# A normalization's root of variance worked out from the one before it, and its scaling given to ACT

## Chip, cores, metric

The kernel runs on one core of one Trainium2 chip. The metric is the device time of one execution in microseconds (us); a version's time is the median of its runs. Engines are named as the profile does: PE (TensorE), DVE (VectorE), ACT (ScalarE), POOL (GpSimd) and SP (SyncE, which here only issues transfers).

## What is computed

The input is 8 batches of 512 tokens with 128 features, float32. Four blocks follow each other: two attentions and two feed-forward parts, each added to its input and then normalized per token. The change touches the first attention alone:

```python
def _layernorm(x, axis=-1, eps=1e-05):
    m = jnp.mean(x, axis=axis, keepdims=True)
    v = jnp.var(x, axis=axis, keepdims=True)
    return (x - m) / jnp.sqrt(v + eps)

# first attention, per batch
q, k, v = jnp.split(jnp.einsum('bsd,ed->bse', x, w_qkv), 3, axis=-1)
att = jax.nn.softmax(jnp.einsum('bqd,bkd->bqk', q, k) * DIM ** -0.5, axis=-1)
y = jnp.einsum('bqk,bvd->bqd', att, v)          # sum over k and, apart from it, over v
h = x + jnp.einsum('bqd,ed->bqe', y, w_fc) + b_fc
a = (h - mean(h)) * rsqrt(var(h) + 1e-5) * gamma + beta   # first normalization
x = _layernorm(x + a)                                      # second
# the next block begins with
h = ln1_scale * (x - mean(x)) / sqrt(var(x) + EPS) + ln1_shift   # third, its scale applied in the next phase
```

The einsum that multiplies att by v sums over k in att and over v in v separately, so y is the row's sum of att times one vector.

## The kernel before

The program is a row of phases, each ended by a barrier; the first, `phase_attention`, works on one batch of 512 tokens (four row blocks of 128, `NT = 4`) per step, eight steps n = 0 to 7, the last two written out behind a loop of three turns with two steps each. Buffers are double by s, the step's parity. Each engine runs its own sequence in the order written; semaphores tie them together.

- SP, per step: waits for `x_free`, issues the load of x for tile n+2, waits for `x1_ready` and stores x1, waits for `z1_ready` and stores z1. A load stands behind the z1 store of the step before it.
- PE, per step n: four scores (`ps[4+i]`, each freed by the exp of the tile before), then `front(n+1)`: four transposes of x (L278), the projections q (L281) and k (L282), then the sum for v (L297) and the output weight (L299).
- ACT, per step: four exps (L319, each waiting for its negated maximum from DVE), `front(n+1)`: xT (L309), q (L311), k (L313); then vsum (L324), then four att (L329), which give only the row sums `attsum` that DVE needs, after waiting for DVE's `rinv`.
- POOL: `norm.root`, that is eps added to four variances per partition (L116) and a power of -0.5 (L119), three times per step; between them `add_bfc` (xb, L247) and `add_beta` (xbeta, L253) for the next tile.
- DVE, `sequence`: `rinv` (L352); maxima 0 and 1 of tile n+1 (L342, L344); h from PSUM (L361); its bn_stats and bn_aggr (L105, L111); maxima 2 and 3; the first normalization `norm.apply` (L132, four instructions of 128x128, one per row block); times gamma (L372); plus xbeta (L374); moments; x1 by `norm.apply`; moments; z1 by `norm.apply`.

`Norm.moments`, `Norm.root` and `Norm.apply` are shared by the phases, so their lines (L105 to L132) occur with the names of several tiles; `a_` marks this phase, and in the profile a_x stands for x1 and for the loaded x, a_h for h and h2, a_z for z1.

## Time and profile before

| | us |
|---|---|
| three runs | 2220.67, 2200.15, 2215.17 (median 2215.17) |
| the profiled execution | 2213.47 |
| its span, first to last instruction | 2212.0 |
| DVE busy | 1324.4 (60%) |
| PE busy | 1545.4 (70%) |
| ACT busy | 1029.8 (47%) |
| POOL busy | 345.8 (16%) |
| first phase: first instruction of the next phase (SP) | 184.03 |

Times in the rows are in us from the span's start; a row of the timeline has start, duration, engine, line, operation, what it writes and reads, shape and count, and in brackets the engine's idle time before it with what ended it. The granted clock (PEclk) is a share of 2.4 GHz. The shares above are means over all phases and say little of the first; its own are read by step.

### The profile page before, as it was taken

How to read it: one execution, taken by the hardware profiler on the slowest of the kernel's cores; microseconds unless marked ns; L12 is line 12 of the kernel's file. 1: busy time of each engine (PE TensorE's matmuls, PEld its weight loads, DVE VectorE, ACT ScalarE, POOL GpSimd, SP SyncE). 2: the span in 40 equal slices, each digit the busy share in tenths (PEclk: the TensorE clock that was granted, in tenths of full speed). 3: DMA queues.
4: the chain of work that ended last, by engine and by line, in shares of the span. 5: the costliest groups of instructions: out<-in, count | busy, mean ns of one | idle time of the engine just before them, and what ended most of it. 6: DMA issues, size and time to landing. Idle time of an engine off the chain costs nothing. (4 is left out here: it accounts for less than half of the span.)

```text
span 2212.0 us, 53944 instructions
## 1 busy us (share of the span) xinstructions
PE 1545.4 (70%) x18859; PEld 988.0 (45%) x19047; DVE 1324.4 (60%) x3180; ACT 1029.8 (47%) x1964; POOL 345.8 (16%) x633
## 2 busy tenths in 40 slices
PE   5532447777722999997525888887878787888447
PEld 2211224444422666664212655555545555555323
DVE  4774277667445676664421766575756575677546
ACT  4332316666700323321414776575757566676203
POOL 2232325555432000000210000000000000000013
PEclk8766659999955999998865999798989898999759
DMA  1114722222146122121888999999999999999442
GB/s 38 43 39 142 235 56 63 62 54 70 29 127 218 51 77 81 52 105 35 245 217 302 334 363 361 351 344 333 344 341 346 336 343 344 338 341 349 126 134 57
DMA packets 194998, 432.92 MB, mean 196 GB/s; under 512 B 37776, under 2 KB 86576, under 8 KB 185360
## 3 DMA queue, kind: packets, MB, share of 16 engines
q1 hardware_dynamic: 171376, 248.53, 36.9%
q10 hardware_dynamic: 12672, 152.05, 16.5%
q0 software_dynamic: 10720, 29.11, 5.1%
q8 instruction: 164, 2.69, 0.5%
q14 instruction: 66, 0.54, 0.1%
HBM read 225.80 MB, written 203.55 MB: 194 GB/s over the span
## 5 line engine op out<-in xcount | busy, mean ns | idle before, releaser
L2083 DVE CUSTOM_DVE_ANT_0 r_shifted<-r_ps_ac,r_shifted 128x512 f32<-128x512 f32 x512 | 352.1, 688 | 319.9 <-PE r_ps_ac L1960 137.1
L2049 ACT ACTIVATE r_probs<-r_ps_keys 128x512 f32<-128x512 f32 x512 | 309.6, 605 | 265.9 <-PE r_ps_keys L1967 233.6
L1967 PE MATMUL r_ps_keys<-r_ident,r_shifted 128*128 128x128 f32 x2048 | 333.0, 288 | 69.6 <-DMA r_v<-v 36.6
L2028 ACT ACTIVATE r_wide<-r_ps_wide 128x512 f32<-128x512 f32 (+1 forms) x576 | 329.7, 591 | 79.4 <-PE r_ps_wide L1951 78.8
L1967 PEld LDWEIGHTS r_ps_keys<-r_ident,r_shifted 128*128 128x128 f32 x2048 | 273.4, 149 | 50.5 <-issue 9.8
L1951 PE MATMUL r_ps_wide<-r_r,r_qv 48*32 48x64 bf16 (+12 forms) x6144 | 239.0, 256 | 62.3 <-issue 49.4
L2091 DVE TENSOR_SCALAR r_shifted<-r_shifted,r_mx 128x512 f32<-128x512 f32 x512 | 249.2, 487 | 18.3
L860 ACT ACTIVATE c_probs<-c_ps_keys 128x512 f32<-128x512 f32 (+1 forms) x384 | 174.7, 530 | 149.6 <-PE c_ps_keys L786 149.4
L1951 PEld LDWEIGHTS r_ps_wide<-r_r,r_qv 48*32 48x32 bf16 x6144 | 103.7, 95 | 165.1 <-issue 163.8
L1427 ACT ACTIVATE e_silu<-e_ps_a 128x1024 f32<-128x1024 f32 x64 | 65.7, 1027 | 216.1 <-PE e_ps_a L1360 216.1
L923 DVE TENSOR_REDUCE c_mx_off<-c_ps_rows 128x2 f32<-128x768 f32 (+2 forms) x192 | 120.8, 686 | 63.7 <-PE c_ps_rows L757 63.7
L1960 PE MATMUL r_ps_ac<-r_k,r_qu 128*128 128x512 bf16 x325 | 134.2, 413 | 34.5 <-issue 27.7
L1978 PE MATMUL r_ps_out<-r_probs,r_v 128*9 128x128 f32 x4096 | 147.7, 281 | 15.2 <-issue 14.5
L124 POOL MEMSET n_norm_consts<- 128x4 f32 x1 | 0.1, 102 | 942.7 <-POOLq L1791 942.7
L757 PE MATMUL c_ps_rows<-c_qk 48*128 48x128 bf16 (+2 forms) x896 | 76.5, 257 | 88.0 <-DVE c_mx_off L923 41.6
L1500 DVE TENSOR_TENSOR e_gu<-e_silu,e_ps_b 128x1024 f32<-128x1024 f32 x64 | 78.2, 1221 | 94.3 <-PE e_ps_b L1360 94.3
L1360 PE MATMUL e_ps_a<-e_hT_half,e_w_half 128*128 128x512 f32 x384 | 125.7, 462 | 4.3 <-DVE e_w_half L1555 4.3
L1960 PEld LDWEIGHTS r_ps_ac<-r_k,r_qu 128*128 128x128 bf16 x512 | 49.4, 97 | 169.4 <-issue 123.6
L891 POOL TENSOR_SCALAR_AFFINE_SELECT c_probs<-c_probs 128x256 f32<-128x256 f32 x256 | 98.4, 409 | 154.5 <-ACT c_probs L860 154.1
L1978 PEld LDWEIGHTS r_ps_out<-r_probs,r_v 128*9 128x9 f32 x4096 | 102.3, 92 | 42.8 <-issue 30.8
L1375 PE MATMUL e_ps_o<-e_weighed,e_w 128*128 128x512 f32 x256 | 120.5, 594 | 0.0
L786 PE MATMUL c_ps_keys<-c_qk 50*128 50x512 bf16 (+3 forms) x512 | 93.8, 311 | 27.5 <-ACT c_probs L860 20.1
(201 smaller groups left out, 2138.0 us busy)
## 6 DMA issues: line engine op xcount, KB each, us to landing
skew<-r_wide ACTq DMA_DIRECT2D x64, 2224.0 KB, 11.9
r_shifted<-skew SPq DMA_DIRECT2D x64, 2048.0 KB, 17.0
e_weight_all<-weights SPq DMA_DIRECT2D x8, 2048.0 KB, 7.6
c_qk<-qk_stacks POOLq DMA_DIRECT2D x64, 192.0 KB, 3.7
stack<-d_part SPq DMA_DIRECT2D x96, 128.0 KB, 2.7
qk_stacks<-b_part SPq DMA_DIRECT2D x48, 128.0 KB, 3.4
qk_stacks<-b_part POOLq DMA_DIRECT2D x48, 128.0 KB, 3.7
stack<-d_part POOLq DMA_DIRECT2D x48, 128.0 KB, 4.0
```

Of the source, the lines that this page charges most:

```text
L860: act.activation(probs[:, p, e, at:at + width], ps_keys[f % BANKS][:, 0:width], ACT.Exp, scale=SCALE)\
L923: last = dve.tensor_reduce(off[:, :, NT * p + b], ps[:, :, at:at + width], AX_X, ALU.max)
L1360: last = pe.matmul(ps[:, k, :], w[a][:, e, k * P:(k + 1) * P], hT_halves[b][:, s, :], start=(i == 0), stop=(i == 2))
L1375: last = pe.matmul(ps_o[s][:, :], w3[:, e, k * P:(k + 1) * P], weighed[:, e % 4, k, :], start=(e == 0 and k == 0), stop=(e == NE - 1 and k ...
L1951: last = pe.matmul(ps[Q * a:Q * a + Q, frm - lo:to - lo], qv[rows, h, q0 + one:q0 + one + Q], r[rows, g // 2, h, at:at + to - frm], start= ...
L1960: pe.matmul(ps_ac[u % 2][:, :], qu[:, s, h, b * P:(b + 1) * P], k[:, s, h, :], start=True, stop=True)\
L1967: last = pe.transpose(ps_keys[u % 2][:, j * P:(j + 1) * P], shifted[:, s, u, j * P:(j + 1) * P], ident[:, :])
L1978: last = pe.matmul(ps_out[Q * b:Q * b + VW, h * P:(h + 1) * P], v9[:, s, j, h * VW:(h + 1) * VW], probs[:, h % 2, j, b * P:(b + 1) * P], s ...
L2028: act.activation(wide[:, s, c, lo:hi], ps_wide[bk % BANKS][:, 0:hi - lo], ACT.Copy).then_inc(wide_sb, 1)
L2049: act.activation(probs[:, h % 2, :, b * P:(b + 1) * P], ps_keys[u % 2][:, :].rearrange("p (j i) -> p j i", j=NT), ACT.Exp, scale=SCALE).th ...
L2083: dve.tensor_tensor_reduce(out=shifted[:, s, u, :], in0=ps_ac[u % 2][:, :], in1=shifted[:, s, u, :], scale=1.0, scalar=LOWEST, op0=ALU.add ...
L2091: dve.tensor_scalar(shifted[:, s, u, :], shifted[:, s, u, :], mx[:, u:u + 1], None, ALU.subtract).then_inc(s_ready, 1)
```

## The change

Let v be the variance that the second normalization finds. Its output x1 has mean 0 and variance v/(v+eps), so the third one's factor per row is 1/sqrt(v * rstd^2 + eps). The new kernel works this out on POOL (`find_factor`: square of rstd, times v, plus eps, power -0.5) and ACT multiplies x1 by it (`scale_rows`, four ACTIVATE with a scale per row), one step later, between vsum and att. DVE's third moments and third apply are gone. The first normalization is now two groups of scalar_tensor_tensor: (h - mean) * gamma, then * rstd + xbeta, each four instructions of 128x128. The second normalization has its own `Norm` object, `norm2`. The maxima stand differently: three before h and the fourth behind the second moments. The first two steps are written out ahead of the loop, which makes two turns.

On DVE, one step from h to its second apply; the names are tiles, a_ps the score banks in PSUM. Before:

```order
L361 SCALAR_TENSOR_TENSOR a_h<-a_ps,a_attsum,a_xb 128x128 x4
L51 ISA
L105 BN_STATS a_norm_stats<-a_h 128x6 x4
L108 ISA
L111 BN_AGGR a_norm_mv<-a_norm_stats 128x2 x4
L341 REGISTER_ALU
L342 TENSOR_REDUCE a_mx<-a_ps 128x1
L344 TENSOR_SCALAR a_negm<-a_mx 128x1
L341 REGISTER_ALU
L342 TENSOR_REDUCE a_mx<-a_ps 128x1
L344 TENSOR_SCALAR a_negm<-a_mx 128x1
L132 TENSOR_SCALAR a_h<-a_h,a_norm_mv,a_norm_rstd 128x128 x4
```

The same place in the changed kernel (second step, written out):

```order
L389 SCALAR_TENSOR_TENSOR a_h<-a_ps,a_attsum,a_xb 128x128 x4
L105 BN_STATS a_norm_stats<-a_h 128x6 x4
L111 BN_AGGR a_norm_mv<-a_norm_stats 128x2 x4
L398 SCALAR_TENSOR_TENSOR a_h<-a_h,a_norm_mv,a_gam 128x128 x4
L405 SCALAR_TENSOR_TENSOR a_h<-a_h,a_norm_rstd,a_xbeta 128x128 x4
L105 BN_STATS a_norm_stats<-a_h 128x6 x4
L111 BN_AGGR a_norm_mv<-a_norm_stats 128x2 x4
L370 TENSOR_REDUCE a_mx<-a_ps 128x1
L372 TENSOR_SCALAR a_negm<-a_mx 128x1
L132 TENSOR_SCALAR a_x<-a_h,a_norm_mv,a_norm_rstd 128x128 x4
```

No maximum stands between the first moments and the first normalization now; the one left behind h (the fourth) comes after the second bn_aggr, and the third has gone ahead of h.

On ACT, from the last exp of a tile to the att of that tile; a_z is the new group. Before:

```order
L319 ACTIVATE a_probs,a_rowsum<-a_ps,a_negm 128x512
L308 REGISTER_ALU
L309 ACTIVATE a_xT,a_xsum<-a_ps 128x512
L310 ISA
L311 ACTIVATE a_qT<-a_ps 128x512
L312 REGISTER_ALU
L313 ACTIVATE a_kT<-a_ps 128x512
L324 ACTIVATE a_vsum<-a_ps 128x128
L329 ACTIVATE a_att,a_attsum<-a_probs,a_rinv 128x512 x4
```

Now:

```order
L337 ACTIVATE a_probs,a_rowsum<-a_ps,a_negm 128x512
L326 REGISTER_ALU
L327 ACTIVATE a_xT,a_xsum<-a_ps 128x512
L328 ISA
L329 ACTIVATE a_qT<-a_ps 128x512
L330 REGISTER_ALU
L331 ACTIVATE a_kT<-a_ps 128x512
L342 ACTIVATE a_vsum<-a_ps 128x128
L356 ACTIVATE a_z<-a_x,a_factor 128x128 x4
L349 ACTIVATE a_att,a_attsum<-a_probs,a_rinv 128x512 x4
```

The order of what was there is the same; four a_z stand in front of att, and they write the tile of the step before.

On POOL, from xb to the factor in the changed kernel's loop:

```order
L251 TENSOR_TENSOR a_xb<-a_x,a_bfc 128x512
L116 TENSOR_TENSOR a_norm_var_eps<-a_norm_mv,a_norm_consts 128x4
L119 TENSOR_TENSOR a_norm_rstd<-a_norm_var_eps,a_norm_consts 128x4
L264 REGISTER_ALU
L265 TENSOR_TENSOR a_factor<-a_norm_rstd 128x4
L51 ISA
L266 TENSOR_TENSOR a_factor<-a_factor,a_norm_mv 128x4
L51 REGISTER_ALU
L267 TENSOR_TENSOR a_factor<-a_factor,a_norm_consts 128x4
L51 REGISTER_ALU
L268 TENSOR_TENSOR a_factor<-a_factor,a_norm_consts 128x4
```

Where a third root stood (L116 and L119 once more) there are now four operations on four columns, the last of them a power.

The diff:

```diff
--- before.py
+++ after.py
@@ -137,7 +137,6 @@
 def phase_attention(nc, sems, x_in, w_qkvT, w_fcT, b_fc, gamma, beta, ident_in, x1_out, z1_out):
 
 
-
     SCALE = P ** -0.5
     with ExitStack() as ctx:
         def sb(name, shape, dt=F32):
@@ -172,7 +171,9 @@
         h2 = sb("h2", [P, NT, P])
         x1 = sb("x1", [P, 2, NT, P])
         z1 = sb("z1", [P, 2, NT, P])
+        factor = sb("factor", [P, 2, NT])
         norm = Norm(ctx, nc, sems, "a_norm")
+        norm2 = Norm(ctx, nc, sems, "a_norm2")
         ps = [ctx.enter_context(nc.psum_tensor(f"a_ps{i}", [P, 512], F32)) for i in range(8)]
 
         consts = sem("consts")
@@ -198,15 +199,18 @@
         marks = sem("marks")
         x1_ready = sem("x1_ready")
         z1_ready = sem("z1_ready")
+        factor_chain = sem("factor_chain")
+        factor_ready = sem("factor_ready")
         stored = [sem("stored0"), sem("stored1")]
         block = sems.block(ctx)
 
         def steps(step, eng):
 
-
-            with eng.Fori(0, NB // 2 - 1) as it:
+            for s in range(2):
+                step(0, s, True)
+            with eng.Fori(0, NB // 2 - 2) as it:
                 for s in range(2):
-                    step(it, s, True)
+                    step(it + 1, s, True)
             for s in range(2):
                 step(NB // 2 - 1, s, s == 0)
 
@@ -253,17 +257,31 @@
                 pool.tensor_tensor(xbeta[:, s, :, :], x[:, s, :, :],
                                    bet[:, :].unsqueeze(1).broadcast_to([P, NT, P]), ALU.add).then_inc(x_free, 1)
 
+            def find_factor(n, s):
+
+                chain = Chain(pool, factor_chain, n, 3)
+                if not isinstance(n, int) or n >= 2:
+                    pool.wait_ge(z1_ready, n - 1)
+                chain.step(pool.tensor_tensor(factor[:, s, :], norm2.rstd[:, :], norm2.rstd[:, :], ALU.mult))
+                chain.step(pool.tensor_tensor(factor[:, s, :], factor[:, s, :], norm2.mv[:, :, 1], ALU.mult))
+                chain.step(pool.tensor_tensor(factor[:, s, :], factor[:, s, :], norm2.consts[:, 0, :], ALU.add))
+                pool.tensor_tensor(factor[:, s, :], factor[:, s, :], norm2.consts[:, 1, :], ALU.pow)\
+                    .then_inc(factor_ready, 1)
+                chain.done()
+
             def step(it, s, ahead):
                 n = 2 * it + s
-                norm.root(pool, 3 * n + 1)
+                norm.root(pool, n + 1)
                 if ahead:
                     add_bfc(n + 1, 1 - s, it + 1 + s)
-                norm.root(pool, 3 * n + 2)
-                norm.root(pool, 3 * n + 3)
+                norm2.root(pool, n + 1)
+                pool.wait_ge(norm2.rstd_ready, n + 1)
+                find_factor(n, s)
                 if ahead:
                     add_beta(n + 1, 1 - s)
 
             norm.constants(pool)
+            norm2.constants(pool)
             pool.wait_ge(consts, 96)
             add_bfc(0, 0, 1)
             add_beta(0, 0)
@@ -322,17 +340,27 @@
                     front(n + 1, 1 - s)
                 act.wait_ge(v_ps, n + 1)
                 act.activation(vsum[:, :], ps[3][:, 0:1].broadcast_to([P, P]), ACT.Copy).then_inc(vsum_sb, 1)
+                if not isinstance(n, int) or n >= 1:
+                    scale_rows(n - 1, 1 - s)
                 act.wait_ge(rinv_ready, n + 1)
                 for i in range(NT):
 
                     act.wait_ge(att_done, NT * n + i + 1)
                     act.activation(att[:, i % 2, :], probs[:, s, i, :], ACT.Copy, scale=rinv[:, i:i + 1],
                                    accum_out=attsum[:, s, i:i + 1]).then_inc(att_done, 1)
+
+            def scale_rows(n, s):
+                act.wait_ge(x1_ready, n + 1)
+                act.wait_ge(factor_ready, n + 1)
+                for t in range(NT):
+                    last = act.activation(z1[:, s, t, :], x1[:, s, t, :], ACT.Copy, scale=factor[:, s, t:t + 1])
+                last.then_inc(z1_ready, 1)
 
             act.sem_inc(p_sb, NT)
             act.sem_inc(att_done, 2)
             front(0, 0)
             steps(step, act)
+            scale_rows(NB - 1, 1)
 
         @block.vector
         def _(dve):
@@ -347,12 +375,12 @@
             def sequence(it, s, ahead):
 
                 n = 2 * it + s
-                chain = Chain(dve, chain_s, n, 4)
+                chain = Chain(dve, chain_s, n, 3)
                 dve.wait_ge(p_sb, NT * (n + 2))
                 dve.reciprocal(rinv[:, :], rowsum[:, :]).then_inc(rinv_ready, 1)
                 if ahead:
-                    maxima(n + 1, 0)
-                    maxima(n + 1, 1)
+                    for i in range(NT - 1):
+                        maxima(n + 1, i)
                 dve.wait_ge(fc_ps, n + 1)
                 dve.wait_ge(xb_ready, n + 1)
                 dve.sem_inc(marks, 1)
@@ -363,22 +391,28 @@
                                                     op0=ALU.mult, op1=ALU.add)
                 chain.step(last)
                 dve.sem_inc(fc_read, 1)
-                norm.moments(dve, h, 3 * n + 1)
+                norm.moments(dve, h, n + 1)
+                dve.wait_ge(norm.var_ready, n + 1)
+                dve.sem_inc(marks, 1)
+                for t in range(NT):
+                    last = dve.scalar_tensor_tensor(out=h2[:, t, :], in0=h[:, t, :], scalar=norm.mv[:, t, 0:1],
+                                                    in1=gam[:, :], op0=ALU.subtract, op1=ALU.mult)
+                chain.step(last)
+                dve.wait_ge(x_free, n + 1)
+                dve.wait_ge(norm.rstd_ready, n + 1)
+                dve.sem_inc(marks, 1)
+                for t in range(NT):
+                    last = dve.scalar_tensor_tensor(out=h[:, t, :], in0=h2[:, t, :], scalar=norm.rstd[:, t:t + 1],
+                                                    in1=xbeta[:, s, t, :], op0=ALU.mult, op1=ALU.add)
+                chain.step(last)
+                if not isinstance(n, int) or n >= 1:
+                    dve.wait_ge(factor_ready, n)
+                    dve.sem_inc(marks, 1)
+                norm2.moments(dve, h, n + 1)
                 if ahead:
-                    maxima(n + 1, 2)
-                    maxima(n + 1, 3)
-                chain.step(norm.apply(dve, h2, h, 3 * n + 1))
-                gm = gam[:, :].unsqueeze(1).broadcast_to([P, NT, P])
-                chain.step(dve.tensor_tensor(h[:, :, :], h2[:, :, :], gm, ALU.mult))
-                dve.wait_ge(x_free, n + 1)
-                chain.step(dve.tensor_tensor(h2[:, :, :], h[:, :, :], xbeta[:, s, :, :], ALU.add))
-                norm.moments(dve, h2, 3 * n + 2)
-
+                    maxima(n + 1, NT - 1)
                 dve.wait_ge(stored[s], 32 * it + 32)
-                norm.apply(dve, x1[:, s, :, :], h2, 3 * n + 2).then_inc(x1_ready, 1)
-                dve.wait_ge(x1_ready, n + 1)
-                norm.moments(dve, x1[:, s, :, :], 3 * n + 3)
-                norm.apply(dve, z1[:, s, :, :], x1[:, s, :, :], 3 * n + 3).then_inc(z1_ready, 1)
+                norm2.apply(dve, x1[:, s, :, :], h, n + 1).then_inc(x1_ready, 1)
                 chain.done()
 
             dve.sem_inc(fc_read, 1)
```

## Rows read from the trace of the kernel before

**Rows 1.** Stretch table, one step: us, then each engine's busy us (instructions), PEclk, DMA.

```profile
107.69:127.31 19.62, 10.66 (x20) 5.01 (x20) 14.46 (x51) 7.75 (x22) 6.12 (x8) 0.65 0.13 42
```

**Rows 2.** Timeline, DVE, one step from h to h.

```profile
107.69 1.13 DVE L361 SCALAR_TENSOR_TENSOR a_h<-a_ps,a_attsum,a_xb 128x128 f32<-128x128 f32 x4 [1.41 <-ACT a_att L329]
...
109.98 0.38 DVE L111 BATCH_NORM_AGGREGATE a_norm_mv<-a_norm_stats 128x2 f32<-128x6 f32 x4
110.28 0.66 DVE L342 TENSOR_REDUCE a_mx<-a_ps 128x1 f32<-128x512 f32 x1
...
111.86 1.97 DVE L132 TENSOR_SCALAR a_h<-a_h,a_norm_mv,a_norm_rstd 128x128 f32<-128x128 f32 x4
113.86 0.69 DVE L372 TENSOR_TENSOR a_h<-a_h,a_gam 128x512 f32<-128x512 f32 x1
...
118.22 1.11 DVE L132 TENSOR_SCALAR a_x<-a_h,a_norm_mv,a_norm_rstd 128x128 f32<-128x128 f32 x4 [1.49 <-POOL a_norm_rstd L119]
...
122.18 2.05 DVE L132 TENSOR_SCALAR a_z<-a_x,a_norm_mv,a_norm_rstd 128x128 f32<-128x128 f32 x4 [1.40 <-POOL a_norm_rstd L119]
...
127.31 1.13 DVE L361 SCALAR_TENSOR_TENSOR a_h<-a_ps,a_attsum,a_xb 128x128 f32<-128x128 f32 x4 [1.41 <-ACT a_att L329]
```

**Rows 3.** Timeline, first and last h of the seven steps, last step's end.

```profile
28.91 1.13 DVE L361 SCALAR_TENSOR_TENSOR a_h<-a_ps,a_attsum,a_xb 128x128 f32<-128x128 f32 x4
...
146.92 1.13 DVE L361 SCALAR_TENSOR_TENSOR a_h<-a_ps,a_attsum,a_xb 128x128 f32<-128x128 f32 x4 [1.44 <-ACT a_att L329]
...
166.81 1.13 DVE L361 SCALAR_TENSOR_TENSOR a_h<-a_ps,a_attsum,a_xb 128x128 f32<-128x128 f32 x4 [2.99 <-ACT a_att L329]
...
181.47 0.33 SPq L236 DMA_DIRECT2D z<-a_z  x1
```

**Rows 4.** Timeline, ACT, the same step.

```profile
111.16 0.69 ACT L319 ACTIVATE a_probs<-a_ps,a_negm 128x512 f32<-128x512 f32 x1 [2.17 <-DVE a_negm L344]
...
111.98 0.69 ACT L319 ACTIVATE a_probs<-a_ps,a_negm 128x512 f32<-128x512 f32 x1
...
112.66 0.59 ACT L309 ACTIVATE a_xT<-a_ps 128x512 f32<-128x512 f32 x1
...
115.50 0.60 ACT L311 ACTIVATE a_qT<-a_ps 128x512 f32<-128x512 f32 x1 [2.16 <-PE a_ps L281]
...
117.70 0.27 ACT L324 ACTIVATE a_vsum<-a_ps 128x128 f32<-128x128 f32 x1
124.35 0.72 ACT L329 ACTIVATE a_att<-a_probs,a_rinv 128x512 f32<-128x512 f32 x1 [6.38 <-DVE a_rinv L352]
```

**Rows 5.** Timeline, POOL, the same step.

```profile
110.44 0.20 POOL L116 TENSOR_TENSOR a_norm_var_eps<-a_norm_mv,a_norm_consts 128x4 f32<-128x4 f32 x1 [6.68 <-DVE a_norm_mv L111]
110.72 1.02 POOL L119 TENSOR_TENSOR a_norm_rstd<-a_norm_var_eps,a_norm_consts 128x4 f32<-128x4 f32 x1
111.71 1.27 POOL L247 TENSOR_TENSOR a_xb<-a_x,a_bfc 128x512 f32<-128x512 f32 x1
```

**Rows 6.** Line L932: its 32 durations (min/median/max ns), and its timeline beside POOL.

```profile
L932 DVE TENSOR_TENSOR c_mx<-c_mx_on,c_mx_off x32: 151/153/357, 304.7 to 587.5; 128x16 f32<-128x16 f32 x32
...
385.28 0.41 POOL L891 TENSOR_SCALAR_AFFINE_SELECT c_probs<-c_probs 128x256 f32<-128x256 f32 x1 [1.90 <-ACT c_probs L860]
...
385.43 0.28 DVE L932 TENSOR_TENSOR c_mx<-c_mx_on,c_mx_off 128x16 f32<-128x16 f32 x1
```

**Rows 7.** Timeline, PE, scores and the transposes behind them.

```profile
118.61 4.96 PE L291 MATMUL a_ps<-a_kT,a_qT 128*128 128x512 f32 x8
127.83 0.86 PE L278 MATMUL a_ps<-a_ident,a_x 128*128 128x128 f32 x4 [4.26 <-DMA a_x<-in_L_attn_x_dram]
```

**Rows 8.** Stretch table of line L291 on PE, six steps: busy, PEclk, DMA.

```profile
97.00:107.60 10.60, 3.60 (x8) 0.98 0.19 69
...
sum 63.70, PE 30.26; mean PE 5.04
```

**Rows 9.** Timeline, SP, the load of x.

```profile
124.83 0.41 SPq L231 DMA_DIRECT2D a_x<-in_L_attn_x_dram  x1
```

## Prediction

> **What bounds the kernel now.** The change touches the first phase alone, which ends 184 of the 2212 us in. I read first its timeline by engine over one step of its loop, from the first h operation of one step (the scalar_tensor_tensor of L361) to that of the next. That is 107.69 to 127.31, 19.6 us [rows 1, 2]; seven such starts lie between 28.91 and 146.92, mean 19.67 [rows 3]. In that stretch DVE is busy 14.5 us, PE 10.7, ACT 7.8 and POOL 6.1 [rows 1]. DVE's idle gaps are those of the normalizations (1.40 to 1.49 us before L132, waiting for POOL's power) and 1.41 before h, waiting for ACT's att [rows 2]. ACT in turn sits 6.38 us idle until DVE's a_rinv [rows 4]. So the step is one chain through DVE: h, three normalizations, the reciprocal, four att on ACT, the next h.
>
> A second ring runs beside it with slack: the last exp of tile n+1 (L319), xT of n+2 (L309), q and k, vsum, att of n+1, h. Called H, the start of h: exp starts at H+4.29, xT at H+4.97, vsum 5.04 after xT [rows 2, 4]. Att could start 0.2 after vsum begins and needs 2.96 to h (124.35 to 127.31): 13.2 us in all against 19.6, so 6.4 us of slack.
>
> **What it removes on DVE.** The third normalization: from the end of a_x (118.22 + 1.11) to the end of a_z (122.18 + 2.05) is 4.9 us [rows 2]. The multiplication by gamma and the addition of beta (0.69 each) go, but the two scalar_tensor_tensor groups that replace them and the first apply are four instructions each of 128x128; the nearest row is h, 1.13 for four and 1.27 to the next group less its wait [rows 2]. One of them (h minus mean, times gamma) now runs while POOL makes the root. Were DVE's chain still what ends a step, this alone would bring it far below 19.6; that is rival E.
>
> **What it moves: the ring's turn.** The fourth maximum of the next tile goes behind the second bn_aggr; the order on ACT is unchanged, so xT, q, k and vsum of the tile after it queue behind the exp of that maximum. With rows: aggregate starts at H+2.29 (109.98), its result is used from about H+2.81; the first new group fills to H+4.08; the root is out at H+4.05 and its user started at H+4.17 (111.86) [rows 2, 5]. The second new group starts at H+4.17, the second aggregate 2.29 later (6.46), the maximum 0.30 after that (110.28 behind 109.98), exp 0.88 later (111.16 behind 110.28; I take the same), xT 0.68 later (112.66 behind 111.98) [rows 2, 4]. So xT starts at H+8.33, not H+4.97, before any contention.
>
> **What contention adds.** With POOL idle an apply of four takes 1.11 us (a_x); beside POOL's 1.27 us xb it takes 1.97 (a_h) and beside xbeta 2.05 (a_z): the first of the four instructions is held until POOL ends [rows 2, 5]. The new groups are of another kind: two SBUF tensors in. One row shows such an instruction under POOL: c_mx, 0.15 us by its median, took 0.28 when it began 0.15 after a POOL operation of 0.41, and ended with it [rows 6]. So they are held too. The first new group starts while POOL runs eps (0.20) and the power (1.02), the second while POOL runs xb (1.27) [rows 5]. No row shows the 1.02 us power beside such an instruction. Bounds: it holds nothing and neither does xb, 0; xb alone holds, 1.97 - 1.11 = 0.86; both hold. For the last I put them in turn, one DVE instruction (0.15 of it after POOL's end) between two of POOL's: eps to 2.95, one DVE to 3.10, power to 4.12, one DVE to 4.27, xb to 5.53, two DVE to 5.95, second group from 6.09 instead of 4.17: 1.9 us. I take 1.9, since each POOL operation for which there is a row, of 0.41 and of 1.27 us, holds to its end. The Trainium skill (SBUF — State Buffer, section Who interferes with whom) states that a DVE instruction with two SBUF inputs contends with a GpSimd one that reads SBUF, and that the second "fully blocks" until the first finishes. It names no exception for a power on four columns; by it the term is 1.9, by the rows alone 0 to 1.9.
>
> So xT at H + 8.33 + 1.9 = H + 10.2.
>
> **From xT to the next h.** Two paths end there. ACT: vsum 5.04 after xT; 0.18 later four new copies a_z of 128x128 with a factor per row. No row has them; vsum (128x128, 0.27) and q (0.60 for four times the columns) give 0.086 per 100 columns, att (0.71 at 512) less 384 columns gives 0.38 each, and as consecutive ones overlap by some 0.1, 1.2 us for four (bounds 0.8 from vsum, 1.5 without overlap). Then 2.96: 5.04 + 0.18 + 1.2 + 2.96 = 9.4. DVE: there are now three maxima ahead of h, and the third waits for the third score of the tile after next. Scores start 5.95 after xT (118.61 less 112.66) and the eight matmuls took 5.04 on average over six tiles, 3.60 in the one with a granted clock of 0.98 [rows 4, 7, 8]. PE idles before and its clock is then at the 1.2 GHz level for the first part; the last score is at the 2.4 GHz level and takes 3.60/4 = 0.90. So the third score is out at 5.95 + 5.04 - 0.9 = 10.1, and the maximum with its scaling needs 0.9: 11.0. Before, only two maxima stood there and their scores had long been done. The later path decides: 11.0, and 9.4 where the clock is full.
>
> One step: 10.2 + 11.0 = 21.2 us against 19.67. DVE then idles some 5 us before its maxima, so that apply against the factor's operations on POOL costs nothing; without that cover it would be 0.9.
>
> **SP's and POOL's queues.** z1's store now waits for ACT's scaling, and the next x load is issued behind it. That scaling ends 4.6 us before h; issue to transposes took 3.0 us (124.83 to 127.83) [rows 7, 9], so the transposes are done near H-1 and are needed at H+10.2: hidden by 11 us. find_factor adds three operations like eps (0.28 apart) and one like the power: 1.95 after the root with DVE's instructions between [rows 5], needed 3 us later in the loop.
>
> **The sum.** First h: +0.8, a third maximum ahead of it. Six steps to the seventh h (of tile 6): 6 x (21.23 - 19.67) = +9.4. Tile 6 to tile 7 has no front: the second root 8.22 + 1.9 after h, factor and its landing 2.1, copies 1.2, att 2.96: 16.4 against 166.81 - 146.92 = 19.9, -3.5. From the last h to the store of z1: the root at 8.22 + 0.8 (power holds, no xb), factor and copies 3.5, total 12.5 against 181.47 - 166.81 = 14.7, -2.2 [rows 3]. Total +0.8 + 9.4 - 3.5 - 2.2 = +4.5 us. The profiled execution took 2213.5 us (span 2212.0), so 2218.0; it lies 1.7 below the median of the three runs, 2215.2, which is less than they differ among themselves (20.5 us).
>
> **The rivals.**
> A, the forecast: both POOL operations hold DVE, scores mostly at the lower clock: 2218. Chance 0.44.
> B, only xb holds (0.86): step 20.2; 0.8 + 3.1 - 4.6 - 3.2 = -3.9: 2209.6. For it: the power touches four columns only. Chance 0.22.
> C, neither holds: step 19.3; 0.8 - 2.0 - 5.5 - 3.2 = -9.9: 2203.6. Against it: c_mx. Chance 0.08.
> D, as A or B but PE's clock is up for the scores, as in one window of six, so that 9.4 stands for 11.0: 6 x 1.6 = 9.6 less: 2200 to 2208. Chance 0.11.
> E, the ring does not bind (the exp of the fourth maximum finds its work early) and DVE's chain sets the step at about 16: 0.8 - 21.6 - 5.7 = -26.5: 2187. Against it: the order of ACT's queue. Chance 0.05.
> F, the other side: the clock stays at 1.2 GHz through the scores, as PE idles longer in each step. Six matmuls at twice 0.45 then put the third score 5.95 + 5.4 = 11.35 after xT, the step is 22.5, +7.5: 2225.5. It decides from the third score being later than 11 us after xT; to be 1% slower (22 us) a step would have to take 24.1 us, which it does not reach alone. Chance 0.10.
>
> Within 1% is about what a measurement of this kernel can tell from no change. A to D and F lie in it, 0.95 of the chance; runs differ by up to 1% and take some of that to either side: faster 0.06, same 0.88, slower 0.06. The range 2200 to 2230 reaches from the fast end of D to beyond F by the spread of runs.
>
> **What would show it.** Right: starts of h 21.2 apart; the first group of scalar_tensor_tensor (L398) stretched to 2 us or more and the second late at H+6.1; xT at H+10.2; DVE idle some 5 us before its maximum on PE's scores; ACT idle only between exps. Wrong: L398 at 1.1 us (B or C), a power on POOL longer than 1.02 in its place (then POOL waits and DVE does not); h released by ACT's att rather than by the third maximum (D); steps under 18 us (E).

## Result: 0.7% slower, and not where the forecast looked

"The relative part" below is the phase of the relative attention together with the projection ahead of it. A "jump back" is TensorE's branch at the end of a turn of a loop; "H+x" is x us after the start of h in a step. In the rows, "<-issue" marks idle time in which the engine waited for nothing that the row can name.

| | before | after |
|---|---|---|
| median of 8 runs, us | 2215.78 (2200.15 to 2220.67) | 2229.02 (2224.41 to 2235.3) |
| ratio, 95% interval | | 1.0074 [1.0051, 1.0097] |
| profiled execution, its span | 2213.47, 2212.0 | 2230.08, 2228.6 |
| first instruction of the second phase | 184.03 | 182.25 |
| step of the first phase, mean of six | 19.67 | 20.56 |
| projection and relative attention | 1036.9 | 1056.1 |

The forecast was 2218.0; the kernel takes 13 us more than before instead of 3 to 5. The changed phase even ends 1.8 us earlier. The loss came in code that the diff doesn't touch: the third attention, with relative positions, and the projection ahead of it. The busy times by stretch (the first phase; all up to that projection; it and the relative attention; the rest), first before, then after; columns are PE, PEld, DVE, ACT, POOL busy with counts, the granted PE clock, the DMA share and GB/s:

```profile
1.10:184.00 182.90, 80.41 (x160) 36.65 (x160) 114.61 (x408) 63.56 (x169) 49.05 (x66) 0.71 0.12 40
184.00:1038.20 854.20, 607.30 (x5636) 392.15 (x5637) 521.95 (x951) 318.41 (x577) 239.64 (x469) 0.86 0.31 92
1038.20:2075.10 1036.90, 786.54 (x12773) 518.51 (x12960) 616.92 (x1587) 624.68 (x1185) 26.70 (x50) 0.88 0.93 320
2075.10:2212.00 136.90, 71.20 (x290) 40.69 (x290) 70.95 (x234) 23.17 (x33) 30.16 (x44) 0.69 0.38 111
```

```profile
1.10:182.20 181.10, 79.78 (x160) 37.43 (x160) 88.48 (x328) 72.84 (x201) 52.28 (x84) 0.70 0.12 41
182.20:1037.10 854.90, 609.16 (x5637) 392.45 (x5637) 522.06 (x951) 318.37 (x577) 238.75 (x469) 0.86 0.31 92
1037.10:2093.20 1056.10, 837.69 (x12960) 525.67 (x12960) 616.54 (x1587) 624.89 (x1185) 26.61 (x50) 0.85 0.92 314
2093.20:2228.50 135.30, 69.93 (x290) 40.19 (x290) 70.96 (x234) 23.11 (x33) 30.06 (x44) 0.70 0.38 112
```

In the first phase DVE does 26 us less work (114.61 to 88.48) and ACT 9 more, as the change says, and the phase gains 1.8. In the third stretch DVE, ACT and POOL do the same work in 19 us more. PE's busy time there can't be compared: before's trace lacks 187 matmul records (12773 against 12960, with 12960 weight loads in both). The granted clock of the stretch is 0.88 before and 0.85 after.

**The changed step**, from h to h (111.70 to 132.18), timeline of after, DVE, ACT and POOL's rows that answer to [rows 2, 4, 5] (the last row counts two of h's four instructions, since its window ended there):

```profile
111.70 1.13 DVE L389 SCALAR_TENSOR_TENSOR a_h<-a_ps,a_attsum,a_xb 128x128 f32<-128x128 f32 x4
114.52 1.14 DVE L398 SCALAR_TENSOR_TENSOR a_h<-a_h,a_norm_mv,a_gam 128x128 f32<-128x128 f32 x4
114.73 1.02 POOL L119 TENSOR_TENSOR a_norm_rstd<-a_norm_var_eps,a_norm_consts 128x4 f32<-128x4 f32 x1
115.72 1.26 POOL L251 TENSOR_TENSOR a_xb<-a_x,a_bfc 128x512 f32<-128x512 f32 x1
116.00 1.92 DVE L405 SCALAR_TENSOR_TENSOR a_h<-a_h,a_norm_rstd,a_xbeta 128x128 f32<-128x128 f32 x4 [0.34 <-POOL a_norm_rstd L119]
119.41 0.66 DVE L370 TENSOR_REDUCE a_mx<-a_ps 128x1 f32<-128x512 f32 x1
120.29 0.69 ACT L337 ACTIVATE a_probs<-a_ps,a_negm 128x512 f32<-128x512 f32 x1 [7.78 <-DVE a_negm L372]
120.97 0.59 ACT L327 ACTIVATE a_xT<-a_ps 128x512 f32<-128x512 f32 x1
126.17 1.27 ACT L356 ACTIVATE a_z<-a_x,a_factor 128x128 f32<-128x128 f32 x4
126.92 5.19 PE L309 MATMUL a_ps<-a_kT,a_qT 128*128 128x512 f32 x8
128.92 0.69 DVE L370 TENSOR_REDUCE a_mx<-a_ps 128x1 f32<-128x512 f32 x1 [6.70 <-PE a_ps L309]
131.29 0.69 DVE L370 TENSOR_REDUCE a_mx<-a_ps 128x1 f32<-128x512 f32 x1
132.18 0.61 DVE L389 SCALAR_TENSOR_TENSOR a_h<-a_ps,a_attsum,a_xb 128x128 f32<-128x128 f32 x2
```

The ring is the one forecast: ACT sits 7.78 us idle until the fourth maximum, xT follows 0.68 later, the scores 5.95 after it, DVE waits 6.70 us for the first of them, and the third maximum (131.29) is what h stands behind.

**The untouched loop.** TensorE's timeline at one jump back of the relative attention's loop (six turns, five jumps). Before, the jump is at 1527.4:

```profile
1527.29 0.31 PE L1951 MATMUL r_ps_wide<-r_r,r_qv 48*32 48x224 bf16 x6 [1.01 <-issue]
1532.49 0.61 PE L1960 MATMUL r_ps_ac<-r_k,r_qu 128*128 128x512 bf16 x1 [4.89 <-issue]
```

After, at 1538.2:

```profile
1538.08 0.90 PE L1985 MATMUL r_ps_wide<-r_r,r_qv 48*32 48x64 bf16 x20
1544.10 0.61 PE L1994 MATMUL r_ps_ac<-r_k,r_qu 128*128 128x512 bf16 x1 [5.12 <-issue]
1550.20 0.59 PE L1985 MATMUL r_ps_wide<-r_r,r_qv 48*32 48x224 bf16 x5 [2.16 <-issue]
```

Both stall some 5 us at the jump. The trace has TensorE's branch itself lasting 4.91 us there before (L1843) and 5.72 us after (L1877). After stalls a second time, 1.9 to 2.3 us at each of the five jumps, ending 11 to 13 us behind it; before doesn't. Queue 8 carries instructions in packets of 16 KB (2.69 MB in 164), and has five more in after, as many as the loop has jumps back. Its row before and after:

```profile
q8 instruction: 164, 2.69, 0.5%
```

```profile
q8 instruction: 169, 2.77, 0.5%
```

So the suspicion for the experiments: the diff writes two more steps out ahead of the first phase's loop, TensorE's compiled program grows there by 82 instructions, and every later loop stands 82 places further on, so at another point of a packet. (An instruction takes 64 bytes if 256 of them fill a packet of 16,384; e5 below bears that out.)

### The profile page after: what moved, and what is told of

It reads as the page before. It is cut to its first block and busy times, and to the rows that moved or that the text cites. A ratio compares the mean times of both kernels' runs of the same rounds, so it can differ in the third digit from the quotient of the medians.

```text
span 2228.6 us, 54057 instructions
## 1 busy us (share of the span) xinstructions
PE 1596.6 (72%) x19047; PEld 995.7 (45%) x19047; DVE 1298.1 (58%) x3100; ACT 1039.2 (47%) x1996; POOL 348.0 (16%) x651
## 5 line engine op out<-in xcount | busy, mean ns | idle before, releaser
L2001 PE MATMUL r_ps_keys<-r_ident,r_shifted 128*128 128x128 f32 x2048 | 339.5, 292 | 12.5 <-issue 6.4
L2001 PEld LDWEIGHTS r_ps_keys<-r_ident,r_shifted 128*128 128x128 f32 x2048 | 276.7, 151 | 63.8 <-issue 18.6
L1985 PE MATMUL r_ps_wide<-r_r,r_qv 48*32 48x96 bf16 (+12 forms) x6144 | 239.5, 259 | 48.9 <-issue 32.0
L1994 PE MATMUL r_ps_ac<-r_k,r_qu 128*128 128x512 bf16 x512 | 214.0, 418 | 62.6 <-DMA r_v<-v 33.5
L2012 PE MATMUL r_ps_out<-r_probs,r_v 128*9 128x128 f32 x4096 | 153.7, 288 | 28.1 <-issue 27.4
```

Source lines behind the costliest of these rows:

```text
L1985: last = pe.matmul(ps[Q * a:Q * a + Q, frm - lo:to - lo], qv[rows, h, q0 + one:q0 + one + Q], r[rows, g // 2, h, at:at + to - frm], start= ...
L1994: pe.matmul(ps_ac[u % 2][:, :], qu[:, s, h, b * P:(b + 1) * P], k[:, s, h, :], start=True, stop=True)\
L2001: last = pe.transpose(ps_keys[u % 2][:, j * P:(j + 1) * P], shifted[:, s, u, j * P:(j + 1) * P], ident[:, :])
L2012: last = pe.matmul(ps_out[Q * b:Q * b + VW, h * P:(h + 1) * P], v9[:, s, j, h * VW:(h + 1) * VW], probs[:, h % 2, j, b * P:(b + 1) * P], s ...
```

## Experiments

Ratios are to runs of the kernel before on the same chip, taken together with them. A relative part or a step is read from one profiled execution of each kernel; those of e1 and e12 were the slowest of their kernel's runs. "Places" is how far TensorE's code behind the first phase stands from where it is in the kernel before. The unit of moving is a semaphore increment that nobody waits for (0.15 us each on TensorE: 128 of them took from 1.1 to 20.6 us in e3).

**Is it the change at all?** e1 is the changed kernel once more; e2 is the kernel before with only its first two steps written out (82 places).

```diff
-            with eng.Fori(0, NB // 2 - 1) as it:
+            for s in range(2):
+                step(0, s, True)
+            with eng.Fori(0, NB // 2 - 2) as it:
                 for s in range(2):
-                    step(it, s, True)
+                    step(it + 1, s, True)
```

> The changed kernel once more, unaltered, beside the kernel before on one chip. In its first profile the first phase ended 1.8 us earlier than before (182.25 against 184.03) and the phase of the relative attention (with the projection ahead of it) took 1056 instead of 1037 us, though none of its lines is changed. Theory P (placement: the longer code of the first phase shifts the code behind it, and the relative attention, whose instructions are fetched while the DMA engines are full, pays for it): the first phase again ends near 182.3, the relative attention again takes 1050 us or more, and the whole is 12 to 19 us above the kernel before. Theory J (chance: the relative attention takes anything between 1037 and 1056 whatever kernel it is in): the whole comes out within 5 us of the kernel before as often as not.

> The kernel before with one part of the change alone: the first two steps of the first phase are written out ahead of its loop, which makes two turns instead of three. No instruction that runs is added or removed but the loop's own. Theory P: the code behind moves about as far as in the changed kernel, so the relative attention takes 10 to 20 us longer and the whole is 10 to 20 us slower, with the first phase still at 184. Theory W (the slower part comes with what the first phase does, not with where code lies): no difference, within 3 us.

e1: 1.0063 [1.0035, 1.0092]. e2: 1.007 [1.0044, 1.0097], its first phase ends at 181.7 and the relative part takes 1053.3 us. Writing out two steps, with the arithmetic unchanged, costs as much as the whole change.

**Only the place.** e3 puts 128 increments ahead of the first phase, e9 82 behind TensorE's last matmul of it, e5 256 there (16 KB in all).

```diff
             steps(step, pe)
+            for i in range(82):
+                pe.sem_inc(pad[i % 2], 1)
```

> The kernel before with 128 semaphore increments on PE ahead of its first wait, where PE is idle until 8.3 us. They shift PE's code of all later phases and change nothing else. Theory P with PE's code as what matters: the relative attention's time moves by 5 us or more either way. Theory W: no difference, within 3 us.

> The kernel before with 256 semaphore increments behind PE's last matmul of the first phase, where PE is idle for some 30 us. At 64 bytes each they shift PE's later code by 16384 bytes, the size of the packets in which the trace shows PE's code coming (164 of them before, 169 in the changed kernel, in the peeled one and with 128 increments). Theory P, sharpened (what matters is where PE's loop of the relative attention lies in blocks of 16 KB: it needs one block more in each turn, and PE runs dry once more behind each jump back): a whole block changes nothing, so relative attention and projection take 1037 us as before (within 4), and the whole is within 4 us of the kernel before. Theory Q (any longer code, or the increments themselves, slows it): 1050 us or more, the whole 15 us or more above.

> The kernel before, with 82 semaphore increments behind TensorE's last matmul of the first attention and nothing else: TensorE's later instructions stand as many places further on as the change puts them, but the first attention's work is that of before. If the place of TensorE's instructions costs the relative attention its time: the first phase ends at 184 to 186 as before, the relative part (with the projection ahead of it) takes 1050 to 1067 us instead of 1037, and the kernel is 14 to 28 us slower than before. If something that the change does in the first phase (its new ACT and POOL work, when it ends, what it leaves in memory) costs it: the relative part stays at 1035 to 1038 us and the kernel within 3 us of before. In the runs so far five kernels with TensorE's later code moved by 82 to 210 places had 1052 to 1067 us, and five that stood as before or a whole 256 places further on had 1033 to 1037.

(e9's text says 82 to 210 places; the furthest of those runs was 128.) e3: 1.0165 [1.0109, 1.0222], but 12.6 us are its increments at the start; the relative part has 1051.7. e9: 1.0079 [1.0053, 1.0106] with the first phase over at 181.5; the relative part 1053.5 us. e5: 1.0035 [1.0015, 1.0054], relative part 1036.6 as before; 7.1 us of its span are increments that outlast TensorE's idle time, and 5.5 us lie in the phases between (the projection's stores and the causal attention). The third stretch of e9, and the same jump in it (1528.0):

```profile
1036.30:2089.80 1053.50, 837.48 (x12960) 525.15 (x12960) 616.41 (x1587) 624.86 (x1185) 26.61 (x50) 0.85 0.92 315
```

```profile
1534.49 0.60 PE L1963 MATMUL r_ps_ac<-r_k,r_qu 128*128 128x512 bf16 x1 [5.68 <-issue]
1540.32 0.59 PE L1954 MATMUL r_ps_wide<-r_r,r_qv 48*32 48x224 bf16 x5 [1.89 <-issue]
```

The stretch reads like that of after (1056.1, 837.69, 314 GB/s), and the second stall is there. 82 increments in idle time, with all arithmetic as before, reproduce the loss; 256 don't.

**What about the place?** e13 to e15 (40, 200, 230 increments, one execution each, so only their profiles count), e16 (40 again, timed), e17 (150).

> The kernel before with 40 increments behind TensorE's last matmul of the first attention. Theory: what counts is where the loop of the relative attention (3486 TensorE instructions of 64 bytes, 13.6 packets of 16 KB) begins within a packet: begun early enough it touches 14 packets, begun later 15, and each packet too many costs a stall at each jump back. A loop of 13.6 packets touches a 15th in about 6 of 10 positions. Then the relative part takes either 1033 to 1038 us with 165 or fewer instruction packets of queue 8, or 1050 and more with 169 or more, nothing between, and of this kernel and the one with 200 increments one is fast and the other slow. If any shift that isn't a whole 16 KB costs, all three of this call are slow.

> The same with 200 increments. By the packet theory it is slow (1050 us and more in the relative part, 169 or more packets) where 40 increments are fast, and fast (1033 to 1038, 165) where 40 are slow. By the rival that any shift costs, slow.

> The same with 230 increments: 26 places short of a whole packet. By the packet theory fast (relative part 1033 to 1038 us, 165 packets) unless the loop of the kernel before begins less than 26 places into its packet (16 to 97 is what the runs so far leave, so about 1 in 8 for slow). By the rival that any shift costs, slow.

> The kernel of e13 again, timed in three rounds. Its one look had 1048.0 us in the relative part, with as many instruction packets as at a fast position, and a second stall of TensorE of 1 to 2.4 us at three of the five jumps back. If the stall is set by how much of the first packet is left behind the jump's target (at 82 increments it begins 4 us after the first stall's end and lasts 2.2 us, at 128 1.4 us and 4.5 us), this position is in between by nature: relative part 1042 to 1050 us, kernel 6 to 12 us above before. If e13 was a chance disturbance of that execution, the part is back at 1033 to 1038 and the kernel within 4 us of before (40 increments lie in TensorE's idle time).

> The kernel before with 150 increments behind TensorE's last matmul of the first attention. By the rule of what is left of the first packet: the second stall begins right behind the first (under 1 us of work between them; 1.4 us with 128, 4 us with 82) and lasts 5 to 6 us, until 12 us after the jump as in e3; 169 packets or more; relative part 1052 to 1067 us, kernel 14 to 28 us above before. If the packets' number alone set it, the stall is that of e9 (2.2 us).

| places | kernels | relative part, us | second stall, us | packets in q8 |
|---|---|---|---|---|
| 0 | before | 1036.9 | none | 164 |
| 40 | e13, e16 | 1048.0, 1047.5 | 0.9 to 2.4 at 3 and 4 jumps | 165, 167 |
| 82 | after, e1, e2, e4, e9 | 1056.1, 1066.9, 1053.3, 1058.9, 1053.5 | 1.4 to 3.0 at all 5 | 169 |
| 128 | e3 | 1051.7 | 4.3 to 5.4 at all 5 | 169 |
| 150 | e17 | 1037.0 | none | 164 |
| 152 | e18 | 1041.2 | none | 164 |
| 200, 230 | e14, e15 | 1033.5, 1037.1 | none | 165, 165 |
| 256 | e5 to e8, e11 | 1033.2 to 1037.3 | none | 165 |
| 256 | e10, e12 | 1033.9, 1044.2 | 0.9 to 1.7 at 2 | 165 |

A second stall counts here if it lasts 0.9 us or more and begins 5 to 13 us behind the jump (shorter ones of 0.7 to 0.8 us occur at 40 and 256 places). Single gaps of 1 to 2.3 us further on (17 to 20 us) occur in the fast kernels too, before among them. In time: e16 1.0052 [1.0005, 1.0099], e17 1.0031 [0.9986, 1.0076]. The packet theory as written fell twice: at 40 places the part is slow without five more packets, and 150 is fast where slow was expected. What holds is the place of the jump's target within its packet: between 128 and 150 places the target passes into the next packet and the stall is gone.

The kept traces name the wait more closely, by two counts that can be taken from their records of TensorE's instructions and of queue 8's packets. First, the second stall comes at a fixed instruction: the 61st record behind the jump at all 25 jumps of the five executions with 82 places, the 15th at all five of e3 (128 places), the 103rd in e13 and e16 (40 places), the 143rd where it occurs at 256 places. That is 143 less the places moved, each time, so it moves by exactly one instruction per place, whatever else the kernel does. The gaps further on are 256 or 512 records behind that point: the 399th at 256 places, the 425th in e15 (230), the 455th in e14 (200). Second, a packet of queue 8 lands just before TensorE goes on: each second stall ends 1.3 to 1.6 us after a packet's end, and each branch at a jump back 1.2 to 2.1 us after one, in all 20 profiled executions. So TensorE runs dry where the target's packet ends, and the second stall is the wait for the next one. Since that packet lands 8 to 12 us behind the jump wherever the boundary lies, a boundary that is reached earlier costs more: the stall ends 10 to 13 us behind the jump (11.1 to 12.5 in e3, 11.6 to 13.1 in e9). A lone gap of 1.7 us in e17, which begins 13.1 us behind its first jump, follows no packet and isn't explained by this.

The first rows behind the jump of e3 (at 1545.1) and of e17 (at 1530.2, which has no second one):

```profile
1551.43 0.61 PE L1963 MATMUL r_ps_ac<-r_k,r_qu 128*128 128x512 bf16 x1 [5.60 <-issue]
1557.61 0.62 PE L1954 MATMUL r_ps_wide<-r_r,r_qv 48*32 48x32 bf16 x8 [4.72 <-issue]
```

```profile
1535.07 0.61 PE L1963 MATMUL r_ps_ac<-r_k,r_qu 128*128 128x512 bf16 x1 [4.46 <-issue]
```

**The change at a good place.** e6 is the changed kernel with 174 increments (256 places), e8 the same with the third maximum behind the first moments, e4 the changed kernel with its four maxima where they were (82 places), e7 e4 with 174 increments. The diff is e4's; e8 moves the third maximum alone and leaves the fourth.

```diff
-                    for i in range(NT - 1):
+                    for i in range(2):
                         maxima(n + 1, i)
...
                 norm.moments(dve, h, n + 1)
+                if ahead:
+                    for i in range(2, NT):
+                        maxima(n + 1, i)
...
-                if ahead:
-                    maxima(n + 1, NT - 1)
```

> The changed kernel with 174 such increments at the same place; with the 82 instructions by which the change lengthened PE's code they make 256. Theory P: the relative attention goes back to about 1037 us, the first phase stays at 182, and the whole is what the change itself is worth, 0 to 5 us below the kernel before. Theory W (the change slows the relative attention by what it does): the whole stays at 2229.

> The changed kernel with the third maximum behind the first moments instead of ahead of h, the fourth where the change put it, and the 174 increments. My account of the step (xT 9.28 after h, then 11.2 to 11.5 for the third score and its maximum; without it ACT's path of 9.33): h is released by att, the step falls from 20.5 to 18.6 us, and the first phase ends 11 to 13 us earlier, at 169 to 171. Rival (the third maximum only waited for something else that ends at the same time): the step stays above 20.

> The changed kernel with the maxima of the next tile in their places of before: two ahead of h, two between the first moments and the first normalization; all else as changed. My theory of the step (the fourth maximum behind the second moments holds ACT's exp, xT and PE's projections, and the third maximum ahead of h waits for the third score): xT comes back to about 5 us after h, and the step falls from 20.5 us to 14 to 16.5; the first phase ends 30 to 45 us earlier than 182, at 140 to 152. Rival (DVE's own work or contention with POOL sets the step): the step stays above 19 us. The whole then is some 35 us below the changed kernel, whichever way the relative attention goes.

> The changed kernel with the maxima in their places of before (first phase 159.7 in its profile) and the 174 increments. Theory P: 15 to 20 us below the same kernel without them (2208), so 2188 to 2193, 1% below the kernel before.

e6: 1.0019 [0.9999, 1.0039]; relative part 1035.2. Against after's 1.0074 that is 12 us back, with the first phase ending 2.7 us later than after's, by its increments (I had expected it 0 to 5 us below before; it is 2.9 above, which can't be told from no change). e8: 1.0022 [1.0, 1.0044]: the step stays at 20.3 to 20.8 instead of the expected 18.6. Two things took the gain back. xT still waits for the fourth maximum and comes 0.6 later (H+9.8 to 10.3), as the third now stands in DVE's chain; and h isn't released by att but stands behind the second maximum, which waits for the second score just as the third had waited for its own (it starts at 130.13, h at 131.01, 10.55 after xT). e4: 0.9973 [0.9947, 0.9999] with the relative part at 1058.9; the step is 16.5 to 17.0 and the phase ends at 159.7 (expected 14 to 16.5, and 140 to 152: the direction was right, the gain smaller). e7: **0.9884 [0.9844, 0.9924]**, 2189.25 us against 2215.55, relative part 1033.2: faster than both kernels. One step of e4 on DVE:

```profile
112.04 1.13 DVE L389 SCALAR_TENSOR_TENSOR a_h<-a_ps,a_attsum,a_xb 128x128 f32<-128x128 f32 x4 [1.20 <-ACT a_att L349]
114.77 0.66 DVE L370 TENSOR_REDUCE a_mx<-a_ps 128x1 f32<-128x512 f32 x1
115.56 0.69 DVE L370 TENSOR_REDUCE a_mx<-a_ps 128x1 f32<-128x512 f32 x1
116.40 1.99 DVE L401 SCALAR_TENSOR_TENSOR a_h<-a_h,a_norm_mv,a_gam 128x128 f32<-128x128 f32 x4
128.80 1.13 DVE L389 SCALAR_TENSOR_TENSOR a_h<-a_ps,a_attsum,a_xb 128x128 f32<-128x128 f32 x4 [3.27 <-ACT a_att L349]
```

The fourth maximum is at H+3.5 instead of H+7.7, and DVE waits 3.27 us for att, not for scores. The places of two maxima had cost the phase 22.5 us (182.25 less 159.7). e8 shows that the third alone is worth nothing; the fourth alone wasn't run.

**What x + b costs.** e10 is e6 with POOL's x + b moved behind the second power; e12 does this to e11; e11 is e7 with its increments divided between two idle stretches of TensorE.

```diff
                 norm.root(pool, n + 1)
+                norm2.root(pool, n + 1)
                 if ahead:
                     add_bfc(n + 1, 1 - s, it + 1 + s)
-                norm2.root(pool, n + 1)
```

> The changed kernel with 174 increments behind TensorE's last matmul of the first attention (as e6) and POOL's x + b moved from between its two power sets to behind the second, where no DVE instruction that reads two operands from SBUF stands beside it. If x + b is what stretches DVE's second scaling to 1.92 us: that operation takes 1.1 to 1.15, the normalization to x_T comes 0.8 us earlier only if DVE's chain and not the fourth maximum sets it; since the fourth maximum stands behind this scaling on DVE, its exponent comes at h + 7.8 instead of h + 8.6, x_T at h + 8.4 instead of 9.3, the step takes 19.6 to 19.8 instead of 20.5, and the kernel is 5 to 6 us faster than e6, 0 to 2 us faster than before minus the increments. If the stretch came from the power set or from the scaling's own operands, it stays at 1.9 and the step at 20.5.

> The changed kernel with the four maxima where the kernel before has them (as e4 and e7) and the 174 increments divided, 124 behind TensorE's last matmul of the first attention and 50 at the start of the projection that follows, where TensorE waits for its weights. The relative part at 1033 to 1037 us as in e7, the step at 16.5 to 17.0. If the increments of e7 were partly exposed, the first phase ends at 159.5 to 160 instead of 161 and the kernel takes 2186 to 2189; if e7's 2189 holds them in full, nothing changes.

> e11 with x + b moved behind POOL's second power set. DVE's first scaling (1.99 us beside x + b in e4) goes to 1.13, and since factor, z, the scaled probabilities and h follow from DVE's chain there, every step gets 0.8 to 0.9 shorter: 15.7 to 16.0 instead of 16.5 to 17.0, the first phase 6 us shorter, the kernel 2180 to 2184. If ACT's own work sets that step instead, it stays at 16.5 and the kernel at e11's time.

e10: 0.9984 [0.9963, 1.0006]. From its timeline:

```profile
107.93 1.14 DVE L408 SCALAR_TENSOR_TENSOR a_h<-a_h,a_norm_rstd,a_xbeta 128x128 f32<-128x128 f32 x4 [0.35 <-POOL a_norm_rstd L119]
111.98 1.26 POOL L252 TENSOR_TENSOR a_xb<-a_x,a_bfc 128x512 f32<-128x512 f32 x1
112.12 0.59 ACT L330 ACTIVATE a_xT<-a_ps 128x512 f32<-128x512 f32 x1
112.13 1.97 DVE L132 TENSOR_SCALAR a_x<-a_h,a_norm_mv,a_norm_rstd 128x128 f32<-128x128 f32 x4 [0.72 <-POOL a_norm_rstd L119]
```

The second scaling is back at 1.14 us and xT at H+8.5 (from 9.3), as expected; the stretch went to a_x, where nothing waits. Its steps are 20.0 to 20.4 in three cases and 17.7 to 17.9 in three others, where the scores ran with the clock up; two score stretches of e10, slow and fast:

```profile
97.30:103.40 6.10, 6.10 (x10) 2.75 (x11) 2.35 (x5) 5.27 (x16) 0.00 (x0) 0.60 0.26 86
117.60:121.30 3.70, 3.68 (x9) 1.44 (x8) 2.41 (x6) 3.70 (x12) 0.00 (x0) 1.00 0.45 144
```

At 1.00 the third maximum begins 8.4 us after xT instead of 10.9, and h follows 9.3 after xT: rival D's time (9.4), in three steps of six, though its sign is missing, as h still stands right behind the third maximum (its scaling starts at 121.23, h at 121.39) and not behind att. Why the clock was up there and not in after isn't settled.

e11: 0.9917 [0.9888, 0.9947]. Its first phase ends at 157.7 against e7's 161.05, but its time of 2195.17 lies above the 2186 to 2189 that I gave: dividing the increments shows no gain over e7. e12: 0.9909 [0.9876, 0.9943], no gain (2193.59, expected 2180 to 2184), and its steps are 0.2 longer (16.7 to 17.3). There the factor is on the path. POOL works in order, so x + b now delays it:

```profile
122.43 1.01 POOL L119 TENSOR_TENSOR a_norm_rstd<-a_norm_var_eps,a_norm_consts 128x4 f32<-128x4 f32 x1
123.41 1.26 POOL L252 TENSOR_TENSOR a_xb<-a_x,a_bfc 128x512 f32<-128x512 f32 x1
124.63 0.20 POOL L266 TENSOR_TENSOR a_factor<-a_norm_rstd 128x4 f32<-128x4 f32 x1
```

1.26 us put in front of the factor takes more than the 0.86 that DVE gets back. I had counted the gain and not the queue.

**The place rule on a kernel that it wasn't found on.** e18 is e4 with 70 increments (152 places).

> The changed kernel with the four maxima where the kernel before has them, and 70 increments behind TensorE's last matmul of the first attention, so that TensorE's later code stands 152 places behind where it is in the kernel before. The place rule, fitted on seven places (40, 82 and 128 slow, 0, 150, 200, 230 and 256 fast), says fast on a kernel that it wasn't fitted on: relative part 1033 to 1038 us, no second stall behind the jumps back, first phase ending at 159 to 160, kernel 2183 to 2190. If the place isn't it, the part takes 1052 us or more as in e4, and the kernel 2205 to 2212.

0.9913 [0.9882, 0.9945], e4 was at 0.9973. No second stall, 164 packets, relative part 1041.2 instead of 1058.9. The direction holds; the part is 3 us above the range given, and the total (2198.03 against 2216.31) above the 2183 to 2190 that I gave.

## Why the prediction failed, step by step

- **"The change touches the first phase alone."** This is the step that failed. True of the arithmetic, not of the time: the sum put the other phases at nothing without a reason, and the 1037 us of the relative part took 19.2 more. e9 and e2 show it without the change's arithmetic, e6 shows the change without it. None of the rivals named it, though each phase's loop stands behind the written-out steps in TensorE's code.
- **DVE's power contention** (A, 1.9 us). Wrong, B was right: L398 takes 1.14 us beside a 1.02 us power and L405 1.92 beside x + b. The Trainium skill (SBUF — State Buffer, Who interferes with whom) states that a DVE instruction with two SBUF inputs contends with a GpSimd one that reads SBUF. The traces agree beside x + b (1.92, 1.99; e10 1.14 without it), and not beside the power on four columns, which reads SBUF too: there the measurement decides against the 1.9 us that the forecast took. xT came at H+9.27, where 8.33 + 0.86 gives 9.2 and the forecast 10.2: this term was 1 us a step too large.
- **xT to h**, forecast 11.0: 11.21 in the step shown, 11.2 to 11.5 over six. Scores 5.95 after xT, as forecast. Four copies 1.27 (forecast 1.2), factor 1.84 (1.95).
- **The step**: forecast 21.2, B 20.2, measured 20.56. Six of them cost 5.4 us instead of 9.4. First h +0.35 (forecast +0.8); tile 6 to 7 15.30 us against 19.89 (-4.6, forecast -3.5); last h to z store 11.75 against 14.66 (-2.9, forecast -2.2). Sum +0.35 + 5.4 - 4.6 - 2.9 = -1.8, forecast +4.5.
- **The ring, not DVE's chain, binds.** Right: e4 puts the two late maxima back and gets 16.5 to 17.0 us per step, rival E's 16.
- **D**, the clock up in the scores: not in after; in e10, at 17.7 to 17.9 us a step.
- **SP's and POOL's queues hidden.** Right: no wait of the transposes appears.
- The total of 2229.0 lies in the range (2200 to 2230) by luck, from two errors of opposite sign: 6 us too much in the first phase, 17 to 19 too little behind it.

**Open.** Five second stalls are 11 us of after's 19.2. The rest, and why e3's 24 us of stalls cost the part only 15, isn't explained; TensorE isn't the only engine that the loop waits for. Part of the rest may be TensorE's clock: its granted share in the relative part was 0.852 in after and 0.877 before. Over all kernels it was 0.844 to 0.861 with second stalls at 40 to 128 places and 0.855 to 0.877 in the others, so the two overlap, and no run separates them. The phases between the first and the relative part vary too: they took 852.6 to 855.4 us in the six executions at 82 and 128 places, 854.1 in before, and 857.1 to 865.2 in the eleven at 150 to 256. The 5.5 us that e5 lost and nearly 4 of e6's lie there. Their cause is open; the packet rule alone doesn't give it, since by that rule 256 places would read like none. Only part of the 256 positions was tried.

## What to carry over

Before costing an edit, ask which loops stand behind it in each engine's code: writing out steps or adding instructions moves them all, and a long TensorE loop may lose or gain by its place: here 1 to 3% of its own time (1047.5 to 1066.9 us against 1033.2 to 1044.2), and up to 0.8% of the kernel. So compare a change with a version moved by idle increments before judging it; here a change that was 0.7% slower by 1.0074 came to 1.0019 [0.9999, 1.0039], which can't be told from no change. And when work is put off on one engine, look who queues behind what it releases: here two maxima of 0.7 us each, put elsewhere, made a step of 16.7 us one of 20.6.

## What the runs showed of the hardware that was not expected

- At a jump back of a loop of some 3485 TensorE instructions, TensorE stands 3.3 to 7.3 us in every kernel, until 1.2 to 2.1 us after a 16 KB packet of instructions has landed. A second stall of up to 5.4 us follows when the target has only some 15 to 103 instructions before the end of its packet; it begins at that end and stops 10 to 13 us behind the jump. With 143 left (0 and 256 places) it was seen at 6 of 40 jumps, 0.8 to 1.7 us long.
- 82 idle semaphore increments, hidden in TensorE's idle time, made the kernel 0.79% slower.
- A power on 128x4, 1.02 us on POOL, doesn't slow DVE instructions with two SBUF operands (1.14 us for four); an add on 128x512, 1.26 us, does (1.92).
